# Peridynamic weighted sum: unread identity turns into the PSUM bank ahead of each spread of the first half

## The chip, the cores and the metric

One core of one Trainium2 chip. The metric is the device time of one launch of the whole program, in microseconds. The kernel before was timed three times; its median is 4004.06 us.

## The reference, cut to what matters

The program is a decoder of four layers with three sublayers each, all in float32. The change is inside one sublayer, the attention of layer 2, a "peridynamic" attention with 16 heads of 8 channels and a horizon of 64 positions. For batch b, position t, head h and distance j it has a bond logit and a damage logit. The part around the change computes

```
s[b,t,j,h]  = logits[b,t,j,h] - 10 * sigmoid(damage[b,t,j,h] + b_dmg_out) + mask[t,j]
w[b,t,j,h]  = softmax over j of s
out[b,t,h,:] = sum over j of w[b,t,j,h] * value[b, t-63+j, h, :]      (8 channels)
Y = out @ W_cproj
```

with 4 batches of 256 positions, 64 distances, 16 heads. The sum over j is what the changed lines help to compute.

## The kernel before, in words

The engines work from queues of their own and meet at counters (semaphores). The function is `peridynamic_gather`. Tokens are in eight tiles of 128 positions; a **half** is four tiles, that is two batches.

The softmax weights of a tile are made by VectorE (DVE), ScalarE (ACT) and GpSimd (POOL). TensorE (PE) then turns them, 128 columns at a time, so that the pairs (distance, head) lie on partitions (`wT`). For the first four tiles this is done by `turn` (L3297) ahead of the loop. For the last four tiles the four turns of one bank are a **late** item (L3334), worked in among the others by the table `LATE_AT`; eight late items in all.

The weighted sum runs over 64 units, 32 for each half, from `units` (L3244): half, block of eight distances `jb` from 7 down to 0, parity `o`, group `q`. A unit has two **spread** items, r = 0 and 1. A spread (L3344) is one float32 matmul, recorded as two LDWEIGHTS and two MATMULs. It takes 32 partitions of `wT` (partitions 0, 32, 64 or 96 on, by q and r) and repeats each weight over its eight channels into a bank of `ps_w`, with 512 columns for jb = 7 down to 400 for jb = 0, 456 on average. DVE multiplies the bank with the shifted values into `prod` (L3491) and frees the bank. There are four banks, so item i waits until item i-4 was taken (`bank_taken` or `late_taken`). Two units, four spreads, make one step p. `add(p)` (L3360) sums the eight products of the step over partitions into `ps_o`: 16 float32 matmuls of 32 rows by 32 columns of the array, recorded as 32.

The order on PE is: the spreads of step 0; then for each p the spreads of step p+1, the late items of that step, and `add(p)`. PE works in order, so a spread that waits holds everything behind it. Between its products DVE also makes four maxima (L3496, in steps 2 to 5) and four sums with reciprocals (L3461 and L3463, in steps 9 to 12) for the weights of the second half. The first half is steps 0 to 15, the second 16 to 31. When the first half's sums are out, ACT copies them (L3416) and PE multiplies with W_cproj (L3320) in step 19.

While PE waits for the weights of the fourth tile it makes 40 unread turns of the identity (`FILL`, L3306).

The line that the change goes in front of, and its wait:

```
if i >= 4 and items[i - 4][0] == "late":
    pe.wait_ge(late_taken.sem, late_taken.nth(late.index(items[i - 4]) + 1))
elif i >= 4:
    pe.wait_ge(bank_taken.sem, bank_taken.nth(by_dve.index(items[i - 4]) + 1))
```

Of the kernel before, what the change touches and what calls it, by code (L numbers as in the profile page):

```python
# [26 lines left out]
P = 128  # L27
# [3172 lines left out]
def peridynamic_gather(m, mask, b_out, weights, damage, value):  # L3200
# [11 lines left out]
    with ExitStack() as ctx:  # L3212
# [8 lines left out]
        ps_w = place.psum("ps_w", [P, 4, BANK])  # L3221
# [24 lines left out]
        PER = NU // 2  # L3246
# [20 lines left out]
        def first(jb):  # L3267

            return J - JB - JB * jb
# [14 lines left out]
        @block.sync  # L3284
        def _(sp):
            sp.dma_start(spread[:, :, :], m.dram["L2_attn_spread2"]).then_inc(small_in.sem, 16)
            sp.dma_start(ident4[:, :], m.dram["L2_attn_ident4"]).then_inc(small_in.sem, 16)
            for c in range(4):
                sp.dma_start(Wc[32 * c:32 * c + 32, :, :], m.dram["L2_attn_W_cproj"].rearrange("(r p) d -> p r d", p=32))\
                  .then_inc(small_in.sem, 16)  # L3290

        @block.tensor
        def _(pe):
            def turn(n, t, k, bank):
                for b in range(4):
                    jb = 4 * k + b
                    mm = pe.transpose(ps_w[:, bank, b * P:(b + 1) * P],  # L3297
                                      weights[:, t, jb * JB:(jb + 1) * JB, :].rearrange("p j h -> p (j h)"), m.ident[:, :])
                mm.then_inc(w_turned.sem, 1)

            for t in range(HALF):
                if t < HALF - 1:
                    pe.wait_ge(weight_pool.sem, weight_pool.nth(t + 1))
                else:
                    for i in range(FILL):
                        pe.transpose(ps_o[:, 0, 0:P], m.ident[:, :], m.ident[:, :])  # L3306
                    pe.wait_ge(weight_dve.sem, weight_dve.nth(1))
                for k in (1, 0):
                    n = 2 * t + 1 - k
                    if n >= 4:  # L3310
                        pe.wait_ge(wT_act.sem, wT_act.nth(n - 3))
                    turn(n, t, k, n % 4)
            pe.wait_ge(small_in.sem, small_in.nth(16 * 6))
            pe.wait_ge(wT_act.sem, wT_act.nth(NT))

            def final(half, bank):
                pe.wait_ge(sum_taken.sem, sum_taken.nth(4 * half + 4))
                for t in range(4):
                    for r in range(4):
                        mm = pe.matmul(ps_w[:, bank, t * P:(t + 1) * P], sums[:, r, t * P:(t + 1) * P], Wc[:, r, :], start=(r == 0),  # L3320
                                       stop=(r == 3), skip_group_check=True)
                return mm

            def emit(i):
                kind, n, r = items[i]
# [4 lines that stand above are left out]
                if kind == "late":  # L3330
                    pe.wait_ge(weight_pool.sem, weight_pool.nth(n))
                    for c in range(4):
                        jb = 4 * r + c
                        mm = pe.transpose(ps_w[:, i % 4, c * P:(c + 1) * P],  # L3334
                                          weights[:, n, jb * JB:(jb + 1) * JB, :].rearrange("p j h -> p (j h)"), m.ident[:, :])
                elif kind == "final":
                    mm = final(n, i % 4)
                else:
                    half, jb, o, q = units[n]
                    if n == PER and r == 0:  # L3340
                        pe.wait_ge(late_taken.sem, late_taken.nth(len(late)))
                    t0 = first(jb)
                    row = slice(64 * q + 32 * r, 64 * q + 32 * r + 32)
                    mm = pe.matmul(ps_w[:, i % 4, 0:2 * (T - t0)], spread[row, o, :],  # L3344
                                   wT[row, jb, half * BANK:(half + 1) * BANK].rearrange("p (b t) -> p b t", b=2)[:, :, t0:],
                                   start=True, stop=True)
                mm.then_inc(bank_made.sem, 1)

            def add(p):
                pe.wait_ge(bank_taken.sem, bank_taken.nth(by_dve.index(("spread", 2 * p + 1, 1)) + 1))  # L3350
                if 2 * p == PER:
                    pe.wait_ge(sum_taken.sem, sum_taken.nth(4))
                for n in (2 * p, 2 * p + 1):
                    half, jb, o, q = units[n]
                    t0 = first(jb)
                    for s in range(2):
                        c = 2 * (n % 2) + s
                        for r in range(4):
                            row = slice(32 * r, 32 * r + 32)
                            mm = pe.matmul(ps_o[32 * c:32 * c + 32, r, :].rearrange("p (b t) -> p b t", b=2)[:, :, t0:],  # L3360
                                           ident4[row, :], prod[row, n % RING, s, :, 0:T - t0], start=(n % PER < 2),
                                           stop=(n % PER >= PER - 2), skip_group_check=True)
                mm.then_inc(added.sem, 1)

            for i in range(begins[0], begins[1]):
                emit(i)
            for p in range(NU // 2):
                if p + 1 < NU // 2:
                    for i in range(begins[p + 1], begins[p + 2]):
                        emit(i)  # L3370
                add(p)
            pe.wait_ge(bank_taken.sem, bank_taken.nth(len(by_dve)))
            final(1, 0).then_inc(y_ready.sem, 1)
# [1177 lines left out]
```

## Time and profile before

| what | us |
|---|---|
| median of 3 runs (lowest to highest) | 4004.06 (4003.64 to 4008.41) |
| time of the profiled execution | 4009.42 |
| its span, first to last instruction | 4007.4 |
| PE busy over the span | 3463.6 (86%) |
| DVE busy | 2608.8 (65%) |
| ACT busy | 1963.6 (49%) |
| POOL busy | 1266.1 (32%) |
| mean granted TensorE clock | 0.907 |
| first half of the weighted sum, first spread to first spread of the second half | 68.2 (2103.0 to 2171.2) |
| second half, to the last add | 47.6 (2171.2 to 2218.8) |

Times in the trace are microseconds from the start of the span. A granted clock of 1.00 is 2.4 GHz, 0.50 is 1.2 GHz. Sublayers follow one another with a barrier, so a microsecond won or lost at the end of this sublayer's chain is one of the whole program. Of matmuls the profile knows the starts; their ends are modelled, and a busy PE need not be streaming all the time.

### The profile page before, as it was taken

To read this page: it belongs to the slowest core of one execution; us is meant where nothing else is said; L and a number is where in the kernel's file an instruction comes from. 1 tells how busy PE (TensorE), PEld (TensorE's weight loads), DVE (VectorE), ACT (ScalarE), POOL (GpSimd) and SP (SyncE) were. 2 spreads that over 40 slices of the span, in tenths; PEclk is the share of its full clock that TensorE was granted. 3 is DMA by queue.
4 is the path that set the end of the run, shared out by engine and by line. 5 is a ranking of instruction groups with operands and counts; after the bars stand their busy time and mean duration, and the time that the engine had idled before them with its cause. 6 is when DMAs were issued, how large, how long until landed. Compare 5 with 4: busy or idle time off the path is not lost. (4 is left out here: it accounts for less than half of the span.)

```text
span 4007.4 us, 96204 instructions
## 1 busy us (share of the span) xinstructions
PE 3463.6 (86%) x40498; PEld 2399.0 (60%) x40498; DVE 2608.8 (65%) x4494; ACT 1963.6 (49%) x3525; POOL 1266.1 (32%) x842
## 2 busy tenths in 40 slices
PE   7566797999999997789959668999999979999996
PEld 4545665777777775732323345666666656666674
DVE  5124484666666666288877777888888857665563
ACT  1122344555555553468861235656666654255552
POOL 1101204555555553400021236666666621000000
PEclk9577898999999998899978889999999998699997
DMA  1021401000000002700000211111111101000000
GB/s 40 5 70 58 146 1 38 2 9 2 9 1 1 1 1 57 255 6 1 1 5 1 61 63 35 52 53 36 52 53 38 30 15 48 9 19 11 11 1 11
DMA packets 88726, 131.40 MB, mean 33 GB/s; under 512 B 18450, under 2 KB 60106, under 8 KB 87532
## 3 DMA queue, kind: packets, MB, share of 16 engines
q1 hardware_dynamic: 85292, 119.03, 10.4%
q8 instruction: 324, 5.31, 0.6%
q0 software_dynamic: 3008, 6.23, 0.4%
q14 instruction: 102, 0.84, 0.1%
HBM read 86.63 MB, written 10.94 MB: 24 GB/s over the span
## 5 line engine op out<-in xcount | busy, mean ns | idle before, releaser
L2773 POOL TENSOR_TENSOR wide_probs<-wide_probs,wide_factor 128x1024 f32<-128x1024 f32 x128 | 239.6, 1893 | 311.1 <-ACT wide_factor L2734 311.1
L2280 ACT ACTIVATE narrow_probsT<-narrow_ps_t 128x512 f32<-128x512 f32 (+1 forms) x448 | 233.0, 566 | 207.8 <-PE narrow_ps_t L2184 205.4
L175 POOL TENSOR_TENSOR model_Y<-model_Y,model_X 128x512 f32<-128x512 f32 x12 | 15.2, 1269 | 996.4 <-POOLq L66 996.4
L2730 ACT ACTIVATE wide_probs<-wide_ps_s,wide_nm 128x1024 f32<-128x1024 f32 (+1 forms) x256 | 237.2, 926 | 172.6 <-DVE wide_nm L2815 152.9
L3185 PE MATMUL bonds_ps<-bonds_act_of,bonds_out 128*32 128x448 f32 (+3 forms) x1024 | 280.9, 568 | 25.1 <-ACT bonds_rows L3168 18.6
L2184 PE MATMUL narrow_ps_t<-narrow_Q,second_KQ 32*128 32x256 f32 (+1 forms) x1664 | 291.9, 410 | 3.0 <-ACT narrow_probsT L2280 2.8
L2335 DVE TENSOR_REDUCE narrow_part<-narrow_ps_s 128x1 f32<-128x512 f32 x384 | 236.1, 683 | 85.6 <-PE narrow_ps_s L2167 85.6
L2810 DVE TENSOR_REDUCE wide_nm<-wide_ps_s 128x1 f32<-128x1024 f32 x128 | 156.0, 1219 | 195.3 <-PE wide_ps_s L2616 195.3
L3919 POOL TENSOR_TENSOR local_turn<-local_turn 128x1024 f32<-128x1024 f32 x96 | 226.7, 2368 | 156.1 <-DVE local_turn L3977 155.4
L2167 PE MATMUL narrow_ps_s<-second_KQ 32*128 32x512 f32 x768 | 255.8, 674 | 18.2 <-issue 16.0
L3134 DVE TENSOR_TENSOR bonds_strain<-peri_in_moved 128x1664 f32<-128x1664 f32 (+3 forms) x128 | 257.4, 2086 | 5.4 <-ACT bonds_act_of L3157 4.4
L2628 PE MATMUL wide_ps<-model_ident,wide_probs 128*128 128x128 f32 (+1 forms) x1664 | 238.9, 274 | 10.8 <-DVE wide_probsT L2820 9.1
L2184 PEld LDWEIGHTS narrow_ps_t<-narrow_Q,second_KQ 32*128 32x128 f32 (+1 forms) x1664 | 210.6, 186 | 35.2 <-ACT narrow_probsT L2280 21.3
L2820 DVE COPY wide_probsT<-wide_ps 128x512 f32<-128x512 f32 x256 | 173.7, 686 | 83.9 <-PE wide_ps L2628 82.9
L2616 PE MATMUL wide_ps_s<-wide_KQ 64*128 64x512 f32 (+1 forms) x1024 | 213.9, 534 | 9.9 <-ACT wide_probs L2730 8.9
L2628 PEld LDWEIGHTS wide_ps<-model_ident,wide_probs 128*128 128x128 f32 (+1 forms) x1664 | 193.1, 139 | 42.5 <-DVE wide_probsT L2820 13.6
L3185 PEld LDWEIGHTS bonds_ps<-bonds_act_of,bonds_out 128*32 128x32 f32 x1024 | 84.6, 111 | 216.6 <-issue 180.5
L3928 POOL TENSOR_TENSOR local_turn<-local_turn,local_ss 128x1024 f32<-128x1024 f32 x96 | 184.0, 1917 | 83.0 <-ACT local_ss L3863 83.0
L3800 PE MATMUL local_ps<-e_wqkv,local_xs 128*128 128x512 f32 x384 | 193.1, 627 | 4.9 <-DVE local_xs L3951 4.3
L2640 PE MATMUL wide_ps<-wide_probsT,wide_V 128*64 128x128 f32 (+1 forms) x3328 | 195.9, 275 | 0.9 <-DVE wide_probsT L2820 0.9
L2640 PEld LDWEIGHTS wide_ps<-wide_probsT,wide_V 128*64 128x64 f32 (+1 forms) x3328 | 180.5, 137 | 5.4 <-DVE wide_probsT L2820 1.1
L3156 ACT ACTIVATE bonds_act_of<-bonds_strain,peri_in_pos 128x832 f32<-128x832 f32 (+3 forms) x128 | 136.3, 1065 | 46.9 <-DVE bonds_strain L3134 31.1
(643 smaller groups left out, 8358.8 us busy)
## 6 DMA issues: line engine op xcount, KB each, us to landing
moe_w<-in_L_ffn_w SPq DMA_DIRECT2D x62, 512.0 KB
local_V<-local_V SPq DMA_DIRECT2D x96, 128.0 KB
e_wqkv<-in_L_ffn_qkv SPq DMA_DIRECT2D x6, 1536.0 KB, 6.8
local_V<-local_V SPq DMA_DIRECT2D x144, 64.0 KB
context_rows<-in_ctx SPq DMA_DIRECT2D x8, 768.0 KB
e_keys<-in_ctx_T SPq DMA_DIRECT2D x6, 800.5 KB, 4.8
e_source<-in_ctx_T SPq DMA_DIRECT2D x4, 800.5 KB, 4.5
second_source<-in_ctx_T SPq DMA_DIRECT2D x4, 800.5 KB, 5.2
```

The source lines that it names most:

```text
L2167: mm = pe.matmul(bank[:, 0:hi - lo], Qh[:, t * P:(t + 1) * P], Kh[:, lo:hi], start=True, stop=True)
L2184: mm = pe.matmul(bank[0:hi - lo, at:at + q1 - q0], KQ_of(s)[part_of(h), lo:hi], Q2[part_of(h), s % RING, q0:q1], start=True, stop=True, sk ...
L2280: act.activation(probsT[0:high, c % PROBS, h, 0:wide], bank[0:high, 0:wide], ACT.Exp).then_inc(t_taken_act.sem, 1)
L2335: dve.tensor_reduce(part[:, s % 2, t, h, piece:piece + 1], bank[:, :], AX.X, ALU.min).then_inc(s_taken.sem, 1)
L2616: mm = pe.matmul(ps_s[h][:, j * BANK:j * BANK + c1 - c0], KQ[rows, s % 2, pair, K + tile * P:K + (tile + 1) * P], KQ[rows, s % 2, pair, c0 ...
L2628: mm = pe.transpose(bank[0:high(c), j * P:(j + 1) * P], probs[:, n % 2, h, c * P:c * P + high(c)], m.ident[:, :])
L2640: mm = pe.matmul(bank[64 * h:64 * h + 64, 0:P], V[0:high(c), s % 2, c, 128 * pair + 64 * h:128 * pair + 64 * h + 64], probsT[0:high(c), n ...
L2730: act.activation(probs[:, n % 2, h, lo:hi], ps_s[h][:, 0:hi - lo], ACT.Exp, bias=nm[:, n % 2, h, 2 * half:2 * half + 1], scale=1.0, accum_ ...
L2773: pool.tensor_tensor(v, v, factor[:, n // 4 % 2, j:j + 1].broadcast_to([P, CUT]), ALU.mult).then_inc(lowered[i].sem, 1)
L3134: dve.tensor_tensor(out, window, here, ALU.subtract).then_inc(strain_dve.sem, 1)
L3185: mm = pe.matmul(ps[32 * c:32 * c + 32, k, half, 0:2 * (T - t0)], out4[:, k, p, :], act_of[:, i % ACTS, k, 2 * half:2 * half + 2, t0:T], s ...
L3919: pool.tensor_tensor(turn1[:, n % 2, j, :, :], turn1[:, n % 2, j, :, :], turn2[:, j, :, :], ALU.add)
```

## The change

In front of each spread of the first half (n below `PER` = 32) PE now turns the 128x128 identity into the first 128 columns of the bank that the spread is about to write. For the first four units (n below 4) it does so three times, for the other 28 once: 8 spreads x 3 + 56 spreads x 1 = 80 turns. Nobody reads them: the spread that follows starts its bank afresh. The turns stand behind the item's wait for its bank and ahead of the spread; no wait is added or removed.

```
                     t0 = first(jb)
                     row = slice(64 * q + 32 * r, 64 * q + 32 * r + 32)
+                    for _ in range(3 if n < 4 else 1 if n < PER else 0):
+                        pe.transpose(ps_w[:, i % 4, 0:P], m.ident[:, :], m.ident[:, :])
                     mm = pe.matmul(ps_w[:, i % 4, 0:2 * (T - t0)], spread[row, o, :],
                                    wT[row, jb, half * BANK:(half + 1) * BANK].rearrange("p (b t) -> p b t", b=2)[:, :, t0:],
                                    start=True, stop=True)
```

On PE, at the start of the first half, the order was (eight spreads, the add of step 0, four spreads; the spread is at L3344 and the add at L3360 before, at L3346 and L3362 after, and the new turn is L3345):

```order
L3297 MATMUL gather_ps_w<-model_ident,peri_logits 128x128 x8
L3344 MATMUL gather_ps_w<-gather_wT,gather_spread 128x512 x8
L3360 MATMUL gather_ps_o<-gather_prod,gather_ident 32x512 x16
L3344 MATMUL gather_ps_w<-gather_wT,gather_spread 128x496 x4
L3360 MATMUL gather_ps_o<-gather_prod,gather_ident 32x512 x16
```

and is now, from the eighth spread on:

```order
L3345 MATMUL gather_ps_w<-model_ident 128x128 x3
L3346 MATMUL gather_ps_w<-gather_wT,gather_spread 128x512
L3362 MATMUL gather_ps_o<-gather_prod,gather_ident 32x512 x16
L3345 MATMUL gather_ps_w<-model_ident 128x128
L3346 MATMUL gather_ps_w<-gather_wT,gather_spread 128x496
L3345 MATMUL gather_ps_w<-model_ident 128x128
L3346 MATMUL gather_ps_w<-gather_wT,gather_spread 128x496
L3345 MATMUL gather_ps_w<-model_ident 128x128
L3346 MATMUL gather_ps_w<-gather_wT,gather_spread 128x496
L3345 MATMUL gather_ps_w<-model_ident 128x128
L3346 MATMUL gather_ps_w<-gather_wT,gather_spread 128x496
L3362 MATMUL gather_ps_o<-gather_prod,gather_ident 32x512 x16
```

No two spreads of the first half stand next to each other any more. At the end of the half, where the second half begins, PE's rows differ from before only by line numbers:

```order
 L3334 MATMUL gather_ps_w<-model_ident,peri_logits 128x128 x8
-L3344 MATMUL gather_ps_w<-gather_wT,gather_spread 128x512 x4
-L3360 MATMUL gather_ps_o<-gather_prod,gather_ident 32x2x200 x16
-L3344 MATMUL gather_ps_w<-gather_wT,gather_spread 128x512 x4
-L3360 MATMUL gather_ps_o<-gather_prod,gather_ident 32x512 x16
-L3344 MATMUL gather_ps_w<-gather_wT,gather_spread 128x496 x4
-L3360 MATMUL gather_ps_o<-gather_prod,gather_ident 32x512 x16
-L3344 MATMUL gather_ps_w<-gather_wT,gather_spread 128x496 x4
+L3346 MATMUL gather_ps_w<-gather_wT,gather_spread 128x512 x4
+L3362 MATMUL gather_ps_o<-gather_prod,gather_ident 32x2x200 x16
+L3346 MATMUL gather_ps_w<-gather_wT,gather_spread 128x512 x4
+L3362 MATMUL gather_ps_o<-gather_prod,gather_ident 32x512 x16
```

The other engines' queues are as before.

## Rows read from the trace of the kernel before

**Rows 1.** Both halves: length, busy us (instructions) of PE, PEld, DVE, ACT, POOL; clock; DMA
```profile
2103.00:2171.20 68.20, 61.50 (x641) 22.30 (x641) 50.82 (x76) 8.79 (x12) 18.81 (x8) 0.75 0.01 1
2171.20:2218.80 47.60, 47.22 (x704) 19.65 (x704) 36.41 (x65) 2.07 (x4) 0.00 (x0) 1.00 0.01 2
```
**Rows 2.** Groups of instructions on DVE, first half (count | busy, mean ns | idle)
```profile
L3491 DVE TENSOR_TENSOR gather_prod<-gather_ps_w,peri_value 128x512 f32<-128x512 f32 (+7 forms) x64 | 36.0, 620 | 22.6 <-PE gather_ps_w L3344 22.6
L3496 DVE TENSOR_REDUCE gather_stat<-peri_logits 128x16 f32<-128x1024 f32 x4 | 7.6, 1892 | 0.0
```
**Rows 3.** Who waited for whom, first half: us in total, times, longest
```profile
DVE gather_prod L3491 <- PE gather_ps_w L3344: 22.6, 11, 8.7
```
**Rows 4.** The same table of stretches, cut where the granted clock changed
```profile
2097.36:2107.60 10.24, 8.67 (x60) 6.08 (x58) 3.47 (x6) 1.08 (x2) 4.56 (x3) 1.00 0.00 0
2107.60:2111.01 3.41, 3.41 (x41) 0.81 (x40) 1.41 (x3) 0.00 (x0) 0.00 (x0) 0.50 0.00 0
2111.01:2121.25 10.24, 8.53 (x100) 2.79 (x112) 9.77 (x13) 1.17 (x2) 4.70 (x2) 1.00 0.01 2
2121.25:2134.91 13.66, 13.66 (x136) 4.39 (x120) 9.65 (x13) 3.06 (x3) 4.70 (x2) 0.50 0.01 1
2134.91:2145.15 10.24, 8.66 (x136) 3.15 (x120) 9.30 (x17) 0.00 (x0) 2.12 (x1) 1.00 0.01 2
2145.15:2162.21 17.06, 16.43 (x164) 6.36 (x133) 13.19 (x20) 1.79 (x3) 7.28 (x4) 0.50 0.01 1
```
**Rows 5.** Timeline of PE: start us, us, line, form, count [idle before]
```profile
2103.00 1.14 PE L3344 MATMUL gather_ps_w<-gather_wT,gather_spread 32*128 32x512 f32 x8 [0.83 <-ACT gather_wT L3384]
2104.88 2.98 PE L3344 MATMUL gather_ps_w<-gather_wT,gather_spread 32*128 32x512 f32 x8 [0.74 <-DVE gather_prod L3491]
...
2119.31 1.65 PE L3344 MATMUL gather_ps_w<-gather_wT,gather_spread 32*128 32x480 f32 x4 [0.46 <-DVE gather_prod L3491]
...
2143.48 1.52 PE L3344 MATMUL gather_ps_w<-gather_wT,gather_spread 32*128 32x432 f32 x4 [1.58 <-DVE gather_prod L3491]
```
**Rows 6.** Timeline of PE at clock 1.00
```profile
2167.80 0.66 PE L3334 MATMUL gather_ps_w<-model_ident,peri_logits 128*128 128x128 f32 x4 [0.63 <-DVE gather_prod L3491]
2168.39 0.95 PE L3360 MATMUL gather_ps_o<-gather_prod,gather_ident 32*32 32x400 f32 x32
...
2171.20 1.14 PE L3344 MATMUL gather_ps_w<-gather_wT,gather_spread 32*128 32x512 f32 x8 [0.83 <-ACT gather_wT L3404]
2172.27 1.02 PE L3360 MATMUL gather_ps_o<-gather_prod,gather_ident 32*32 32x400 f32 x32
...
2175.92 1.14 PE L3360 MATMUL gather_ps_o<-gather_prod,gather_ident 32*32 32x512 f32 x32
2176.99 1.36 PE L3344 MATMUL gather_ps_w<-gather_wT,gather_spread 32*128 32x496 f32 x8
```
**Rows 7.** Timeline of PE at clock 0.50
```profile
2125.89 1.90 PE L3360 MATMUL gather_ps_o<-gather_prod,gather_ident 32*32 32x480 f32 x32
2127.72 2.94 PE L3344 MATMUL gather_ps_w<-gather_wT,gather_spread 32*128 32x464 f32 x8
...
2132.42 1.94 PE L3344 MATMUL gather_ps_w<-gather_wT,gather_spread 32*128 32x464 f32 x8
2134.30 1.34 PE L3360 MATMUL gather_ps_o<-gather_prod,gather_ident 32*32 32x464 f32 x32
...
2149.91 1.11 PE L3334 MATMUL gather_ps_w<-model_ident,peri_logits 128*128 128x128 f32 x4
2150.95 1.74 PE L3360 MATMUL gather_ps_o<-gather_prod,gather_ident 32*32 32x432 f32 x32
```
**Rows 8.** Timeline of PE, the forty unread turns; clock in half-microsecond stretches
```profile
2097.05 4.25 PE L3306 MATMUL gather_ps_o<-model_ident 128*128 128x128 f32 x36
...
2096.50:2097.00 0.50, 0.50 (x4) 0.50 (x3) 0.00 (x0) 0.50 (x1) 0.50 (x1) 0.50 0.00 0
...
2097.50:2098.00 0.50, 0.50 (x7) 0.50 (x6) 0.00 (x0) 0.00 (x0) 0.36 (x2) 1.00 0.00 0
```

More of the change, by code:

```diff
@@ L3343, in emit @@
                     row = slice(64 * q + 32 * r, 64 * q + 32 * r + 32)
+                    for _ in range(3 if n < 4 else 1 if n < PER else 0):
+                        pe.transpose(ps_w[:, i % 4, 0:P], m.ident[:, :], m.ident[:, :])
                     mm = pe.matmul(ps_w[:, i % 4, 0:2 * (T - t0)], spread[row, o, :],
```

## The prediction

> **What bounds the kernel now.** First the two halves of the sum as stretches [rows 1]: the same 64 spreads and 16 adds take 68.2 us in the first half and 47.6 us in the second, although the second also holds the product with W_cproj. DVE is busy 50.8 us of the first, PE is shown busy 61.5 us. On DVE [rows 2] the 64 products are 36.0 us; four maxima of 1.89 us lie between them, and as many sums with reciprocals: with 50.8 us busy in all [rows 1] the sums are left with 50.8 - 36.0 - 7.6 = 7.2 us. About 15 us that the second half does not have. DVE stood idle for 22.6 us before products, always for a spread [rows 3], but 8.7 us of that are the wait for the first one. So neither engine bounds the half alone: they take turns.
>
> The stretches cut at the changes of the clock [rows 4] show 3.4 + 13.7 + 17.1 = 34.1 us of the half at 0.50 (1.2 GHz), the rest at 1.00 (2.4 GHz). What the engine did before each fall stands in the timeline [rows 5]: at 2107.6 four spreads had gone out one at a time (2.98 us for eight matmuls, where the four before took 1.14 us), with no add among them; before 2121.25 and 2145.15 again spreads one at a time, while DVE was at a maximum or a sum. It rose after stretches with an add and four spreads started together, as at 2132.42 [rows 7] before 2134.91.
>
> Last the price of a spread [rows 6]. Four spreads that start together at 2171.20 are over when the add starts at 2172.27: 1.07 us for four, because each uses another quarter of the array's rows. One by itself takes no less. The timeline also shows that a matmul of another tile shape starts only when the one before has streamed out: the add after the turns (2167.80 to 2168.39), the spread after the add.
>
> **The change.** 80 turns are added to PE, nothing to another engine, no wait. Their own length is the small part. A turn uses all 128 rows, so it must wait for the spread in front of it, and the spread behind must wait for the turn. The four spreads of a step, which now overlap wholly or in part, stand in a line.
>
> At clock 1.00. A turn: four take 2167.80 to 2168.39, 0.59 us [rows 6]; a further one in a row costs at most 4.25 / 36 = 0.118 us [rows 8], so one by itself, with the change of shape behind it, 0.59 - 3 x 0.118 = 0.24 us. A spread of 512 columns up to the next shape 1.07 us. An add lasts 1.14 us at 512 columns and 0.95 at 400 [rows 6], 1.7 ns a column; over an average of 456 columns a spread is 1.07 - 0.09 = 0.98 us. Turn and spread 1.22 us, 64 times: 78 us. The 16 further turns of the first eight spreads: 1.9 us. Add to next spread 1.07 us at 512 (2175.92 to 2176.99), 0.98 on average, 15 times before the second half begins: 14.7 us. Eight late items of 0.59 us: 4.7 us. The wait for the last copied turn at 2171.20, [rows 6] 0.83 us, say 1 us. Sum 100 us for what takes 68.2: **+32 us**.
>
> At clock 0.50 [rows 7]. Four spreads together at 464 columns 2132.42 to 2134.30, 1.88 us, at 456 columns 1.85. Four turns 2149.91 to 2150.95, 1.04 us; a further one about 0.2 us (twice the 0.1 of the full clock), so one alone 0.44 us. Turn and spread 2.29 us, 64 times: 147 us. Further turns 3.2 us. Adds 2125.89 to 2127.72, 1.83 us at 480 columns, 1.75 on average, 15 times 26 us. Late items 8.3 us, last wait 1 us. Sum 185 us: **+117 us**.
>
> DVE needs four products (4 x 0.62 us) and at most one maximum or sum (some 2 us) for a step, 4.5 us, where PE now needs 4 x 1.22 + 0.98 = 5.9 us even at the full clock. So DVE's 15 us of maxima and sums, which set much of the half now, are hidden; PE is what is late. POOL and ACT make the weights of the second half behind those sums and have more room than now. The second half has its spreads together again and keeps its 47.6 us, perhaps 2 or 3 us more if it begins at 0.50.
>
> **Which clock.** In the changed first half no two spreads overlap anywhere. Every stretch between adds is of the kind that stood before the three falls, and none is like that at 2132.42. PE being shown busy does not help: 13.66 of 13.66 us from 2121.25 on were at 0.50 [rows 4]. The turns speak for more clock: during the forty unread turns it went from 0.50 to 1.00 [rows 8]; but those were back to back, and here one turn of 0.11 us stands beside a spread of 0.85 us and more. I take the full clock for the first 8 us or so (before, it lasted 4.6 us from the first spread on, and three turns a spread should stretch it), which saves 7 us of the 185, and again for some 6 us at steps 13 to 15, where late items and adds stand together, which saves 5. That makes 173 us, **+105 us**. Against the profiled execution's own 4009.4 us this is 4114; the median of the runs stands 5.4 us lower, so I predict 4004 + 105 = 4109 us.
>
> The Trainium skill has a rule on this in "TensorE: Matmul & The Clock Gate", Part 4 (PE-mode transpose): a transpose does not count as activity, and the full clock does not engage for it. The trace disagrees, with the rise during forty transposes just named. By the rule the added turns could hold no clock at all, the 12 us saved above would fall away, and the time would be 4121; by the trace they help a little.
>
> **The rivals.**
> Serial, but at the full clock. With the turns PE hardly ever stands idle, and in the second half it keeps 1.00 with 47.2 of 47.6 us busy [rows 1]. Then +32 us: 4036; with the clock lost for a third of the time about 4064. Against it speaks the stretch of 13.66 us above. The same page of the Trainium skill, in the table "Why this matters for your kernels", advises to keep TensorE continuously busy so that the clock stays full; by that rule this rival would be right.
>
> Faster. The turn does not hold the neighbouring spreads back (it passes while other rows stream), it fits in the time in which PE waits for DVE, and the clock stays at 1.00. Worth at most what DVE now waits inside the half, 22.6 - 8.7 = 13.9 us [rows 3], less what it would still wait at 1.00. In the second half DVE is idle for 47.6 - 36.4 = 11.2 us [rows 1], the product with W_cproj included; I take 6 of them as the common part: -8 us, 3996. It decides if the serial cost of a turn with its spread stays under the 0.62 us of a product. Against it: every change of shape in rows 6 and 7 waits for the stream before it.
>
> No change. The clock's gain and 80 x 0.118 = 9 us of turns cancel, the turns again not holding the spreads: 4004.
>
> **How the numbers follow.** Forecast 0.66, with a range of its own from 4080 to 4122; serial with most of the clock, 4030 to 4080, 0.25; faster 0.04; no change 0.05. Changes of 0.2%, 8 us, are about what a measurement of this kernel can tell. The bounds of the unknown clock are +32 and +117, which gives 4036 and 4121; I put the range at 4032 to 4122, which leaves out the two cases without serial spreads and the edges. Slower 0.91, same 0.05, faster 0.04.
>
> **What would show it.** The starts of two successive spreads of the first half lie at least 1.1 us apart (2.1 at 0.50), with a turn between; DVE's idle time before products rises from 22.6 to over 90 us, all for the spread; PE is busy throughout; the granted clock is 0.50 for most of a first half of about 170 us; the second half stays within 3 us of 47.6. The forecast is wrong if spreads on different rows still overlap across a turn, or if the stretches show 1.00 through most of the half; then the time is that of the rivals.

## The result, and the profile after

The changed kernel was slower: median 4130.91 us (four runs, 4114.59 to 4134.84) against 4004.11 us before (four runs), a ratio of 1.0306 with a 95% interval of 1.0278 to 1.0335. That is 127 us more, where 105 us more were forecast, and 9 us above the upper end of the range. Measured again on another occasion, beside thirteen runs of the kernel before, it took 4115.07 us (four runs, 4098.76 to 4120.55) against 4011.76 us, a ratio of 1.0240 (1.0179 to 1.0302): 103 us more.

The profiled execution of the first measurement took 4132.82 us, its span is 4131.0 us. The two halves of the sum, as busy time by stretch (length; PE, PEld, DVE, ACT, POOL; clock; DMA share, GB/s), where [rows 1] stood before:

```profile
2112.00:2287.06 175.06, 174.22 (x721) 54.26 (x721) 54.71 (x76) 8.89 (x12) 18.79 (x8) 0.52 0.00 0
2287.06:2334.70 47.64, 47.21 (x704) 19.64 (x704) 36.38 (x65) 2.07 (x4) 0.00 (x0) 1.00 0.01 2
```

The first half, from its first turn to the first spread of the second, is 175.06 us instead of 68.2; the second half is what it was. Cut where the clock changed, as in [rows 4]:

```profile
2107.97:2114.80 6.83, 6.00 (x39) 4.18 (x37) 0.69 (x1) 1.09 (x2) 1.57 (x1) 1.00 0.00 0
2114.80:2254.75 139.95, 139.95 (x557) 40.94 (x556) 47.05 (x63) 5.42 (x6) 18.79 (x8) 0.50 0.00 0
2254.75:2258.16 3.41, 3.41 (x10) 1.25 (x10) 1.38 (x3) 0.00 (x0) 0.00 (x0) 1.00 0.00 0
2258.16:2285.47 27.31, 27.31 (x142) 10.33 (x142) 5.59 (x10) 2.39 (x4) 0.00 (x0) 0.50 0.00 1
```

PE is shown busy for 139.95 of 139.95 us, at half the clock. DVE, grouped by line over the first half, answers to [rows 2], and the waits answer to [rows 3]:

```profile
L3493 DVE TENSOR_TENSOR gather_prod<-gather_ps_w,peri_value 128x512 f32<-128x512 f32 (+7 forms) x64 | 40.2, 628 | 125.0 <-PE gather_ps_w L3346 125.0
L3498 DVE TENSOR_REDUCE gather_stat<-peri_logits 128x16 f32<-128x1024 f32 x4 | 7.4, 1852 | 0.0
```

```profile
DVE gather_prod L3493 <- PE gather_ps_w L3346: 125.0, 56, 10.7
PEld gather_ps_w L3345 <- issue: 81.7, 62, 1.7
```

DVE waits 125.0 us for spreads instead of 22.6, 56 times instead of 11. PE's turns hardly wait for another engine: of 64 groups of turns 62 start after idle time of the weight path that is put down to "issue", that is to PE's own queue, and not to a counter. The other two waited for DVE (2.0 us together); the very first turn also waited 0.83 us for ACT's last copy. The timeline of PE, to be held against [rows 5 to 7]:

```profile
2112.01 0.52 PE L3345 MATMUL gather_ps_w<-model_ident 128*128 128x128 f32 x3 [0.83 <-ACT gather_wT L3386]
2112.46 1.12 PE L3346 MATMUL gather_ps_w<-gather_wT,gather_spread 32*128 32x512 f32 x2
2113.51 0.55 PE L3345 MATMUL gather_ps_w<-model_ident 128*128 128x128 f32 x3
...
2118.05 0.90 PE L3345 MATMUL gather_ps_w<-model_ident 128*128 128x128 f32 x3
2118.89 2.07 PE L3346 MATMUL gather_ps_w<-gather_wT,gather_spread 32*128 32x512 f32 x2
2120.89 0.90 PE L3345 MATMUL gather_ps_w<-model_ident 128*128 128x128 f32 x3
...
2255.55 0.33 PE L3345 MATMUL gather_ps_w<-model_ident 128*128 128x128 f32 x1
2255.82 0.96 PE L3346 MATMUL gather_ps_w<-gather_wT,gather_spread 32*128 32x416 f32 x2
2256.71 0.33 PE L3345 MATMUL gather_ps_w<-model_ident 128*128 128x128 f32 x1
...
2270.59 1.97 PE L3334 MATMUL gather_ps_w<-model_ident,peri_logits 128*128 128x128 f32 x8
2272.49 1.69 PE L3362 MATMUL gather_ps_o<-gather_prod,gather_ident 32*32 32x416 f32 x32
2274.11 0.47 PE L3345 MATMUL gather_ps_w<-model_ident 128*128 128x128 f32 x1
2274.52 1.70 PE L3346 MATMUL gather_ps_w<-gather_wT,gather_spread 32*128 32x400 f32 x2
2276.15 0.47 PE L3345 MATMUL gather_ps_w<-model_ident 128*128 128x128 f32 x1
```

Three turns and a spread of 512 columns take 1.50 us at 1.00 (2112.01 to 2113.51) and 2.84 us at 0.50 (2118.05 to 2120.89). One turn and a spread take 1.16 us at 1.00 and 416 columns, 2.04 us at 0.50 and 400 columns. No spread overlaps another.

The span grew by 4131.0 - 4007.4 = 123.6 us. Of this 106.9 us lie in the first half of the sum (175.06 - 68.2). 9.0 us lie ahead of it: its first instruction starts at 2112.0 instead of 2103.0. 7.8 us lie behind the last add. Instructions in those two parts are the same in both kernels. The largest piece ahead is one stretch in an earlier sublayer, of the kernel before and of the changed one:

```profile
592.00:650.00 58.00, 43.54 (x246) 30.32 (x239) 29.35 (x88) 23.30 (x44) 16.78 (x19) 0.79 0.18 66
```

```profile
592.00:650.00 58.00, 45.38 (x212) 29.57 (x213) 28.97 (x88) 19.17 (x37) 9.68 (x12) 0.65 0.17 66
```

The mean clock there is 0.65 instead of 0.79, and 212 matmuls were done in the time of 246. Followed matmul by matmul, the changed kernel is 0.3 us late at 590 us and 7.5 us late at 620 us. In the second profile of the same changed kernel this stretch had a clock of 0.88, so it is not the change that slows it:

```profile
592.00:650.00 58.00, 42.16 (x253) 29.40 (x251) 31.33 (x91) 24.74 (x47) 16.73 (x19) 0.88 0.17 66
```

### The profile page after: what moved, and what is told of

Its sections match the earlier page's. It is cut to its first block and busy times, and to the rows that moved or that the text cites. A ratio compares the mean times of both kernels' runs of the same rounds, so it can differ in the third digit from the quotient of the medians.

```text
span 4131.0 us, 96364 instructions
## 1 busy us (share of the span) xinstructions
PE 3581.6 (87%) x40578; PEld 2431.4 (59%) x40578; DVE 2614.8 (63%) x4494; ACT 1963.8 (48%) x3525; POOL 1266.3 (31%) x842
## 5 line engine op out<-in xcount | busy, mean ns | idle before, releaser
L3493 DVE TENSOR_TENSOR gather_prod<-gather_ps_w,peri_value 128x496 f32<-128x496 f32 (+7 forms) x128 | 75.9, 626 | 136.6 <-PE gather_ps_w L3346 136.4
```

## The experiments

Each was profiled; "the first half" is the time from the first unread turn or spread of the half to the first spread of the second half. From there to the start of the last matmul of the last add the second half took 47.0 us in all of them; "behind the last add" is the time from that start to the end of the span.

**All turns of a step in one place.** The 80 turns stay, the spreads are next to each other again.

```
-                    for _ in range(3 if n < 4 else 1 if n < PER else 0):
+                    first_of_step = n % 2 == 0 and r == 0
+                    for _ in range(0 if not first_of_step else 12 if n < 4 else 4 if n < PER else 0):
```

> The same 80 unread turns, but all those of a step stand in front of its first spread (12 in each of the first two steps, 4 in each later one), so the four spreads of a step are next to each other again. Theory S (a turn between two spreads takes away their overlap; its own length is small): of the 107 us that the first half gained, only the turns' own length of some 10 to 20 us can remain, so a first half of 75 to 92 us and a time of 4010 to 4030 us. Rival L (the 80 turns cost by their own length and by the clock, wherever they stand): a first half near the 175 us of the changed kernel, 4110 us or more.

4013.4 us against 4013.95 us, ratio 1.0001 (0.9975 to 1.0027). The first half, as busy time by stretch, and PE's timeline of a step:

```profile
2104.47:2168.80 64.33, 59.59 (x721) 26.17 (x721) 50.96 (x76) 8.80 (x12) 18.87 (x8) 1.00 0.01 1
```

```profile
2132.14 0.66 PE L3346 MATMUL gather_ps_w<-model_ident 128*128 128x128 f32 x4
2132.73 1.06 PE L3347 MATMUL gather_ps_w<-gather_wT,gather_spread 32*128 32x464 f32 x8
2133.72 1.16 PE L3363 MATMUL gather_ps_o<-gather_prod,gather_ident 32*32 32x464 f32 x32
```

64.33 us: the same number of turns costs not 107 us but nothing, and the half is even 3.9 us shorter than the 68.2 us of before, below what I expected. In the step shown the four spreads start together and take 0.99 us; where DVE is at a maximum or a sum they still go by ones and twos, as before. The clock is 1.00 throughout, with 34.1 us at 0.50 before. So neither the turns' number nor their length made the loss; their place between the spreads did. Rival L falls.

**Unread work on the rows of the spread.** The turn is replaced by an unread matmul of the spread's own tile shape and row group.

```
-                        pe.transpose(ps_w[:, i % 4, 0:P], m.ident[:, :], m.ident[:, :])
+                        pe.matmul(ps_w[:, i % 4, 0:P], spread[row, o, :], spread[row, o, :], start=True, stop=True)
```

> In place of each unread turn of the identity, an unread float32 matmul of 128 columns on the same 32 rows and 128 columns of the array as the spread behind it, as often (3 and 1). It changes no tile shape and leaves the other three row groups free. It streams twice 128 columns, about twice a turn's. Theory S: spreads of other rows go on overlapping, so the first half stays below 100 us and the time below 4040 us. Rival L (work in front of a spread costs its own length and the clock, whichever rows it uses): 150 us or more for the half.

4007.2 us against 4013.95 us, ratio 0.9995 (0.9972 to 1.0017), first half 65.41 us. The timeline shows a second unread matmul starting before the spread in front of it has ended:

```profile
2111.01 0.58 PE L3346 MATMUL gather_ps_w<-gather_wT,gather_spread 32*128 32x496 f32 x1
2111.27 0.37 PE L3345 MATMUL gather_ps_w<-gather_spread 32*128 32x128 f32 x1
2111.43 0.57 PE L3346 MATMUL gather_ps_w<-gather_wT,gather_spread 32*128 32x496 f32 x1
```

Work in front of every spread is harmless here when it keeps the spread's tile shape and rows. It writes the same bank as the turn did, so the bank is not what makes the others wait; a whole-array instruction in between is. The experiment changes tile shape and rows together and can't tell which of the two counts. A row of the kernel before speaks for the shape:

```profile
2107.78 2.01 PE L3360 MATMUL gather_ps_o<-gather_prod,gather_ident 32*32 32x512 f32 x32
```

This add begins on the 32 rows that the spread at 2104.88 [rows 5] had used, and a spread takes 1.07 us. The last product that it waits for was taken by 2106.67, when the fourth spread was let go. Yet it starts only at 2107.78, 1.11 us behind the start of that fourth spread, which uses other rows. No run tests this by itself.

**A whole-array instruction that streams next to nothing.** Identity as weights, two columns streamed, 64 times.

```
-                    for _ in range(3 if n < 4 else 1 if n < PER else 0):
-                        pe.transpose(ps_w[:, i % 4, 0:P], m.ident[:, :], m.ident[:, :])
+                    for _ in range(1 if n < PER else 0):
+                        pe.matmul(ps_w[:, i % 4, 0:2], m.ident[:, :], m.ident[:, 0:2], start=True, stop=True)
```

> In place of the turns, one unread float32 matmul of the whole identity as weights (128 rows by 128 columns) with only 2 columns streamed, in front of each of the 64 spreads of the first half. It has almost no length of its own in streaming, but the shape of the whole array. Theory S: the loss is in the order that a whole-array instruction forces, so it costs like a turn: a first half of 150 to 185 us, 4090 to 4130 us. Rival L (the turns' streaming is what costs): below 90 us, 4030 us or less.

4128.44 us against 4011.76 us, ratio 1.0290 (1.0232 to 1.0348), first half 179.99 us:

```profile
2154.35 0.59 PE L3345 MATMUL gather_ps_w<-model_ident 128*128 128x2 f32 x2
2154.86 1.96 PE L3346 MATMUL gather_ps_w<-gather_wT,gather_spread 32*128 32x480 f32 x2
2156.76 0.59 PE L3345 MATMUL gather_ps_w<-model_ident 128*128 128x2 f32 x2
```

With next to nothing streamed it costs more than a turn: 2.41 us with its spread at 480 columns, where one turn with its spread took 2.30 us (2147.37 to 2149.67 in the kernel with one turn for every spread, below). The difference lies ahead of the spread, which starts 0.51 us after the unread matmul and 0.41 us after the turn. A float32 matmul of this kind is recorded with two weight loads, 0.50 us of them here, the turn with one of 0.18 us.

**Six turns in front of each spread.**

```
-                    for _ in range(3 if n < 4 else 1 if n < PER else 0):
+                    for _ in range(6 if n < PER else 0):
```

> Six unread turns in front of each of the 64 spreads of the first half, 384 in all instead of 80. Theory S with the clock as its second term (spreads in a line on a quarter of the rows let the clock fall, whole-array turns hold it): at 1.00 one spread with six turns is 0.24 + 5 x 0.11 + 0.98 = 1.77 us, 64 of them 113 us, and 20 us of adds and late turns: a first half of 130 to 137 us, 40 us shorter than with the 80 turns of the change, and about 4090 us. Rival N (turns do not act on the clock, it stays at 0.50): 64 x (0.44 + 5 x 0.2 + 1.85) = 210 us and 35 us for the rest, 245 us and 4190 us or more.

4072.74 us against 4013.95 us, ratio 1.0164 (1.0114 to 1.0214), first half 132.80 us:

```profile
2107.59:2240.39 132.80, 131.97 (x1024) 66.38 (x1025) 54.83 (x76) 8.79 (x12) 18.95 (x8) 1.00 0.00 1
```

```profile
2152.08 0.88 PE L3345 MATMUL gather_ps_w<-model_ident 128*128 128x128 f32 x6
2152.88 1.07 PE L3346 MATMUL gather_ps_w<-gather_wT,gather_spread 32*128 32x480 f32 x2
2153.88 0.87 PE L3345 MATMUL gather_ps_w<-model_ident 128*128 128x128 f32 x6
```

Nearly five times the turns and 42 us less than with the change, as the clock stays at 1.00. The half is as expected; the whole is 17 us below the 4090 expected. In its profile the time behind the last add was 1780.3 us, against 1789.1 in the first profile of the kernel before. One spread with six turns takes 1.80 us (2152.08 to 2153.88) against some 2.3 us with one turn at 0.50. That splits the loss of the change: with the clock held, the lost overlap would be 32 us by the prediction's first sum (the six-turn half less its 384 - 80 = 304 further turns, 0.109 us each or 33 us, is 99.7 us, 31.5 us above 68.2; 0.109 is from the shifted kernel below, where 1020 turns last from 2094.96 to 2206.99 us and 40 in the kernel before from 2096.19 to 2101.13); the other 75 us of the 107 are the clock, which the six turns hold and the one does not. The 68.2 us have 34.1 us at 0.50 in them; against the grouped kernel, all at 1.00 and with the same 80 turns, the lost overlap is 99.7 - 64.3 = 35 us.

**One turn for every spread.**

```
-                    for _ in range(3 if n < 4 else 1 if n < PER else 0):
+                    for _ in range(1 if n < PER else 0):
```

> One unread turn in front of each spread of the first half, for the first four units too: 64 turns instead of 80. Theory S: 16 turns of 0.11 to 0.21 us less, 2 to 4 us, unless the clock falls earlier or later: a first half of 168 to 175 us against the 175 us of the changed kernel. Rival T (the triple turns at the start are what costs): a first half under 150 us.

4114.94 us against 4013.95 us, ratio 1.0249 (1.0190 to 1.0308), first half 171.67 us, 2 and 3 us less than in the two profiles of the change (173.51 and 175.05). The triple turns at the start are not what costs.

**One turn for every second spread.**

```
-                    for _ in range(3 if n < 4 else 1 if n < PER else 0):
+                    for _ in range(1 if n < PER and r == 0 else 0):
```

> One unread turn in front of every second spread (r = 0 only), 32 in all; the spreads go in pairs that may overlap. Theory S: a turn and a pair cost as much as a turn and one spread, 1.22 us at 1.00 and 2.29 us at 0.50. At 1.00 that is 32 x 1.22 + 20 = 59 us, less than VectorE needs, so the half is 64 to 72 us, 100 us less than with turns before every spread; at 0.50 it is 32 x 2.29 + 35 = 108 us. Pairs keep twice as many rows at work as single spreads, so I expect most of it at 1.00 and under 85 us. Rival P (the loss is in proportion to the number of turns): 32 of the 64 turns of the kernel with one each, half of its loss of 103 us, so about 120 us.

4007.5 us against 4012.69 us, ratio 0.9993 (0.9973 to 1.0013). The first half:

```profile
2095.53:2183.89 88.36, 87.03 (x672) 28.50 (x673) 51.79 (x76) 8.90 (x12) 18.85 (x8) 0.65 0.00 1
```

```profile
2124.92 0.47 PE L3345 MATMUL gather_ps_w<-model_ident 128*128 128x128 f32 x1
2125.32 1.92 PE L3346 MATMUL gather_ps_w<-gather_wT,gather_spread 32*128 32x464 f32 x4
2127.17 0.47 PE L3345 MATMUL gather_ps_w<-model_ident 128*128 128x128 f32 x1
```

A turn and a pair take 2.25 us at 0.50, what a turn and one spread took. Half the turns lose 20 us in this profile (88.36 - 68.2), not the half of 103 us that rival P wanted; the clock was at 0.50 for more of it than I expected (61.4 us), so the half is 3 us above the 85 I gave. The median of ten runs shows none of the 20 us; the profiled execution, 4028.95 us, was the slowest of the ten. I can't say from this whether the other runs had a shorter half, or whether the scatter of the rest covers it: only the profiled execution (span 4027.2 us) shows its half.

**Fewer grouped turns.** 4 in front of the first two steps, 2 in front of the others.

```
-                    for _ in range(3 if n < 4 else 1 if n < PER else 0):
+                    first_of_step = n % 2 == 0 and r == 0
+                    for _ in range(0 if not first_of_step else 4 if n < 4 else 2 if n < PER else 0):
```

> Grouped turns again, in front of the first spread of each step only, but 4 in each of the first two steps and 2 in each later one: 36 turns. The grouped kernel with 80 turns had a first half of 64.3 us, all at clock 1.00, against 68.2 us before. Theory S with the clock: if 36 turns still hold 1.00, the half is 61 to 64 us; if they do not, it is the 68 us of before plus up to 4 us of turns, 66 to 72 us. Of the whole program either is under 0.2%, less than its runs differ among themselves, so I expect no difference in the times.

4006.32 us against 4012.69 us, ratio 0.9979 (0.9959 to 0.9998), first half 64.89 us with 10.2 us at 0.50. The half is 3.3 us shorter than 68.2, between the two cases that I gave. The interval of the time just leaves out 1, for 0.2%, in one of several versions tried: at most a hint that this version beats the kernel before.

**The kernel before, shifted.** 1020 unread turns instead of 40 while PE waits for the fourth tile's weights: everything behind comes later, the half itself is as before.

```
-    FILL = 40
+    FILL = 1020
```

> The kernel before, with 1020 unread turns instead of 40 while TensorE waits for the weights of the fourth tile. The 980 further turns last about 980 x 0.109 = 107 us at clock 1.00 and do nothing but push all that follows 107 us back, as the change does. If the rest of the program does not mind being shifted, the time is 4004 + 107 = 4111 us (4108 to 4114), and what the changed kernel takes beyond that (its median is 4131) must come from the change itself. If the part outside the changed half varies by itself with how the granted clock falls on it, this kernel too is off by some 5 to 15 us, in stretches whose instructions are the same, and its runs differ among themselves by as much.

4112.08 us (4110.98 to 4125.9) against 4011.76 us. The median lies where 4004 + 107 had it, while 107 us above its own neighbours would be 4119; the ratio, 1.0256 (1.0197 to 1.0315), allows both. In its profile the first half took 63.72 us, 20.5 us of it at 0.50. The same instructions took 68.2 us elsewhere, so the clock's fall on them is worth 4.5 us by itself, as much as the grouped turns seemed to win. Both profiles of the kernel before have the same clock pattern in the half (34.1 us at 0.50); what differs here is the 107 us of turns ahead of it. That turns inside the half shorten it is therefore not shown.

**Both kernels again.**

> The changed kernel once more, with a second profile. If the 7 us lost near 600 us and the 8 us lost behind the changed half were the change's doing, both stretches are as long here as in the first profile. If they are chance in how the clock falls, the first half of the sum is 175 us again within 3 us, while those two stretches may differ by 5 to 10 us.

4115.07 us against 4011.76 us. First half 173.51 us, and 1797.0 us behind the last add, as in the first profile (1796.9); but the half now began at 2098.9 instead of 2112.0, 4 us earlier than in the first profile of the kernel before. So the 9 us lost ahead of the half in the first profile do not belong to the change; the time behind it did not vary between these two.

> The kernel before once more, with a second profile. If the stretches outside the first half of the sum vary by chance, the granted clock of the stretches around 600 us and behind 3200 us may differ from the first profile; all runs of it shown so far lie within 6 us, so I expect 4003 to 4010 us and a first half of 68 us within 3.

Ten runs from 3992.66 to 4028.09 us, median 4005.94, ratio to its neighbours 0.9990 (0.9959 to 1.0020). First half 68.24 us, 1785.8 us behind the last add (1789.1 in the first profile). The expectation of 4003 to 4010 was wrong for the single runs, though not for the median: three runs had shown 5 us of scatter where there are 35, and the nineteen runs of it beside the first experiments already lay between 3993.4 and 4045.17. Whether the 8 to 11 us behind the sum belong to the change is open: the grouped kernel, without its loss, had 1800.4 us there and the one with six turns 1780.3, so that part varies by 20 us between kernels whose instructions there are the same. It was 1796.9 in the kernel with one turn for every spread, but 1790.0 in the one with two columns, whose half is as long and as slow as that of the change: a long half alone does not bring it.

## Why the prediction was right or wrong

**What bounds, and the change of bound: right.** DVE and PE took turns before; now PE sets every step, DVE waits 125.0 us for spreads ("over 90" was forecast), and its maxima and sums are hidden.

**The price of a turn with its spread: right.** Forecast 1.22 us at 1.00 and 2.29 us at 0.50 for 456 columns. Brought to the columns of the rows: at 416 columns and 1.00 forecast 1.15, measured 1.16 (2255.55 to 2256.71); at 400 columns and 0.50 forecast 2.10, measured 2.04; with three turns at 512 columns and 0.50 forecast 2.88, measured 2.84. Eight late turns 1.90 us (forecast 2.1), an add of 416 columns 1.62 us (forecast 1.61). One reading was off and changed nothing: the sums with reciprocals on DVE, 7.2 us by subtraction, are 7.5 + 1.0 = 8.5 us in the view by line, where neighbouring records overlap a little.

**The clock: right in kind, and the saving was somewhat too large.** I had 14 us of the half at 1.00, the first 8 and 6 near the end. It was 7.8 us: the clock fell 2.8 us after the first turn (2112.0 to 2114.8), came back for 3.4 us at 2254.75, and stood at 1.00 for the last 1.6 us. So the saving of 12 us became some 7, but the prices were a little too high, and the first half came out at 175.06 us where 173 was forecast, 106.9 us more for 105.

**The Trainium skill's rule on transposes** ("TensorE: Matmul & The Clock Gate", Part 4: they do not count as activity). Six turns in front of each spread hold 1.00 for 132.80 us in a place where one turn leaves it at 0.50. The measurement disagrees with the rule, more clearly than the forty turns of [rows 8] did. The advice of the same page of the Trainium skill ("Why this matters for your kernels") to keep TensorE continuously busy was put beside the rival "serial, but at the full clock". It is not enough here: PE is shown busy for 139.95 of 139.95 us, at 0.50.

**The step that failed: the range, and the sum's base under it.** I wrote "the bounds of the unknown clock are +32 and +117, which gives 4036 and 4121", and "the median of the runs stands 5.4 us lower, so I predict 4004 + 105". Both treat the 3940 us outside the half as fixed at what three runs showed, and I took 8 us for what a measurement can tell. The same kernel runs from 3993 to 4045 us when it is run more often, and the stretches outside the half, with equal instructions, differed by up to 16 us ahead of it (the half begins at 2095.5 us in one profile, at 2112.0 in another) and 20 us behind it. In the first measurement they added 9.0 + 7.8 us to the 106.9, and 4130.91 fell outside; in the second, 103 us more than its neighbours, the forecast holds. The 9.0 us are shown not to be the change's; for the 7.8 us it is open. The base was low too: the medians of 13 to 23 runs of the kernel before, on three later occasions, are 4011.76 to 4013.95. The range should have carried 15 us on either side for the rest of the program.

**The rivals.** "Serial at the full clock" did not come about in the change, but it exists: six turns make it, and its 31.5 us agree with the 32 us worked out. "Faster" asked that a turn not hold the neighbouring spreads back; rows and runs exclude it. What it promised from the clock was 8 us; with the overlap kept, the half was 3 to 4 us shorter (64.33 and 64.89), and an unchanged half was as short (63.72). "No change" asked for the same free overlap and falls with it.

## What to carry to other kernels

Before filling idle TensorE time, ask which rows and tile shape the filler uses: here an unread instruction of the whole array between matmuls that share the array by row groups made them run one after the other, even when it streamed two columns. If filler is wanted for the clock, put it in front of a group that runs together, or give it the same tile shape and rows: both cost nothing here, though neither showed a gain in the whole time. And before a forecast of a few per cent is made narrow, find out how much the untouched part varies from run to run; three agreeing runs do not tell.

## What the runs showed of the hardware that I had not expected

More unread work can be faster: 384 turns gave a half of 132.80 us, 80 turns in the same places 175.06 us, because the clock stayed at 1.00.

A whole-array matmul that streams two columns costs a half of 179.99 us against 171.67 us for a turn that streams 128: it has two weight loads in the line where the turn has one.

The granted clock in stretches with the same instructions is not always the same: 0.65 and 0.88 around 600 us in two executions of the changed kernel (0.79 in both of the kernel before), and 34.1 or 20.5 us at 0.50 in an unchanged first half, behind 40 or 1020 turns. In a program of 4000 us that moved parts of it by 5 to 20 us.
